# Sums by src four steps ahead, id loads on ScalarE's queue and four-step loops in a graph kernel's joint stage; bonds ahead of rows in its sort

## The reference

```python
feat_in  = h @ W_in.T + b_in;   feat_out = h @ W_out.T + b_out
a_in  = seg_mean(feat_in[src], dst, N)      # mean over the edges that end at a node
a_out = seg_mean(feat_out[dst], src, N)     # mean over the edges that begin at a node
x = layernorm(x + gru_cell(concat(a_in, a_out), h))
# second layer
m = relu(concat(h[row], h[col], bond) @ W1 + b1) @ W2 + b2
x = layernorm(x + h + segment_sum(m * sigmoid(bond @ Wa + ba), row))
```

## Time and profile before

| | |
|---|---|
| median of three runs | 13765.5 us (13765.47, 13765.5, 13784.85) |
| profiled execution | 13790.1 us, its span 13788.4 us |
| mean granted TensorE clock | 0.751 of full speed |
| busy share: PE, PEld, DVE, ACT, POOL | 63%, 56%, 61%, 20%, 70% |
| `sort_records`, first to last POOL scatter | 2369.1 to 6652.3 us |
| `sum_rest`, first gather to last DVE row | 6675.7 to 8843.2 us |

### The profile page before, as it was taken

How to read it: one execution, slowest core, us unless ns; L and a number is a source line. 1 busy time by engine, 2 the same in 40 slices (tenths; PEclk the granted TensorE clock), 3 DMA queues, 4 the chain that set the end, 5 groups by cost and what they waited for, 6 DMA issues and landing times. The chain is left out here.

```text
span 13788.4 us, 248865 instructions
## 1 busy us (share of the span) xinstructions
PE 8650.6 (63%) x53687; PEld 7661.1 (56%) x53688; DVE 8351.6 (61%) x29389; ACT 2713.3 (20%) x7251; POOL 9705.6 (70%) x10125
## 2 busy tenths in 40 slices
PE   3777776333333333333577777797888888888876
PEld 2555554333333333333577777556777777777775
DVE  6555555666666666666677777554444455444444
ACT  0000000111111111111000000154444444444444
POOL 3777776777777777777777777306777777777774
PEclk9555555555656555666788888898999999999998
DMA  5822223666666666666677777513333334333336
GB/s 178 308 54 54 54 54 84 197 198 196 199 196 199 197 199 196 199 196 199 174 187 186 186 186 186 95 52 76 80 79 79 80 88 94 80 79 80 79 79 82
DMA packets 2665496, 1884.08 MB, mean 137 GB/s; under 512 B 1375795, under 2 KB 2460371, under 8 KB 2664784
## 3 DMA queue, kind: packets, MB, share of 16 engines
q1 hardware_dynamic: 1505269, 806.75, 22.1%
q0 software_dynamic: 377360, 782.89, 19.9%
q10 hardware_dynamic: 782662, 292.60, 8.8%
HBM read 1509.53 MB, written 483.44 MB: 145 GB/s over the span
## 5 line engine op out<-in xcount | busy, mean ns | idle before, releaser
L1846 POOL DMA_INDIRECT p<-q_rows,small x3432 | 3250.1, 947 | 1643.5 <-issue 1000.0
L1051 PE MATMUL bank<-p,ring 128*128 x6656 | 1549.0, 426 | 2714.7 <-DVE ring L972 2711.5
L1051 PEld LDWEIGHTS bank<-p,ring 128*128 128x128 f32 x6656 | 1437.8, 328 | 2826.1 <-issue 2826.1
L1110 POOL DMA_INDIRECT edges_a<-ring,small x1664 | 1635.7, 983 | 563.1 <-issue 441.4
L1110 POOL DMA_INDIRECT edges_b<-ring,small x1664 | 1632.5, 981 | 507.6 <-issue 441.1
L799 POOL DMA_INDIRECT ring<-in_x,ring x1664 | 1573.9, 946 | 533.7 <-issue 530.0
L1884 PE MATMUL bank<-ring 128*128 128x256 f32 x3432 | 1205.4, 437 | 766.4 <-DVE p L1796 766.1
L830 PE MATMUL bank<-ring 128*128 128x129 f32 x3328 | 1240.3, 491 | 617.8 <-DMA ring<-in_x,ring 525.1
L1252 POOL DMA_INDIRECT ring<-in_x,small x1352 | 1278.7, 946 | 463.2 <-issue 411.3
L1272 PE MATMUL bank<-p,ring 128*128 128x129 f32 x8360 | 1194.3, 312 | 525.1 <-DVE ring L1200 525.1
L1272 PEld LDWEIGHTS bank<-p,ring 128*128 128x128 f32 x8360 | 1157.7, 226 | 562.5 <-issue 562.5
(11 more groups left out here) (289 smaller groups left out, 14195.4 us busy)
## 6 DMA issues: line engine op xcount, KB each, us to landing
p<-rows_by_slot SPq DMA_DIRECT2D x418, 928.0 KB
p<-edges_b SPq DMA_DIRECT2D x530, 262.0 KB
p<-edges_a SPq DMA_DIRECT2D x520, 262.0 KB
bonds_by_dst<-in_bond ACTq DMA_DIRECT2D x5, 20625.0 KB, 159.1
ring<-edges_a ACTq DMA_DIRECT2D x1792, 33.0 KB
p<-q_rows,small POOLq DMA_INDIRECT x3432
ring<-edges_b ACTq DMA_DIRECT2D x1664, 33.0 KB
ring<-bonds_by_dst ACTq DMA_DIRECT2D x1672, 32.0 KB
```

The source lines that it names most:

```text
L1051: last = nc.tensor.matmul(found[q][:, j, :], hot_t[g % GRPS][:, QUAD * h + j, :], x, start=True, stop=True, skip_group_check=True)
L1110: pool.indirect_dma_start(out=c.edges[s], out_offset=bass.IndirectOffsetOnAxis(ap=pos[:, k:k + 1], axis=0), in_=rec[:, k, :], in_offset=No ...
L1846: pool.indirect_dma_start(out=gath[g][:, k, :], out_offset=None, in_=c.q_dram, in_offset=bass.IndirectOffsetOnAxis(ap=gidx[g][:, k:k + 1], ...
```

## The change

In the sort, SP's order within a step is turned: the bonds' wait and load come first, then the rows'.

In the joint stage:

- PE and DVE run the sums by src four steps ahead of the sums by dst (`LEAD`): before the loop PE makes `sum_out` of steps 0 to 4, and DVE `add_out` of steps 0 to 3 with the preparations that follow; a turn has `add_in(u)`, `add_out(u + 4)`, `prepare_in(u + 2)`, `prepare_out(u + 6)`.
- PE's and DVE's loops have four steps; the last two turns (eight steps) are written out, without the work that lies beyond step 207.
- DVE loads the block numbers of a step in two parts, eight before `add_in`, five before `add_out`.
- The ids to gather and the places in the block are loaded by ScalarE's queue in two DMAs, the places into four buffers of their own. ScalarE waits for the last gather of step u - 3, then for DVE's `prepare_in(u)`.
- `sum_out` is zeroed by ScalarE (an activation with scale 0). POOL no longer waits for any zeroing.
- SP has only the windows; the two loads of windows past the last step are gone.

```diff
@@ sort_records, SP
                         u = i * LOOK + g
+                        sp.wait_ge(s_sc[2 * (g % GRPS)], i * (2 * QUAD * 16) + g // GRPS * (QUAD * 16))
+                        load_bonds(u, 2 * (g % GRPS))
                         sp.wait_ge(s_hot, u * 4 + 12)
                         load_rows(u + 2, g % 2)
-                        sp.wait_ge(s_sc[2 * (g % GRPS)], i * (2 * QUAD * 16) + g // GRPS * (QUAD * 16))
-                        load_bonds(u, 2 * (g % GRPS))
@@ sum_rest
-    W, AHEAD = D + 1, 5
+    s_blank = c.sem("s_blanked")
+    W, AHEAD, LEAD = D + 1, 5, 4
+    TURNS_S = QSTEPS // TURN_V          # TURN_V = 4
@@ SP
                     for g in range(LOOK):
-                        u = i * LOOK + g
-                        load_windows(u, g % 2, edges)
-                        sp.wait_ge(s_agg_in, u * NI + (IN_0 - (LOOK - AHEAD - 1) * NI))
-                        load_ids(u + AHEAD, (g + AHEAD) % LOOK)
-            for k in range(2):
-                load_windows(QSTEPS + k, k, c.edges[1])
+                        load_windows(i * LOOK + g, g % 2, edges)
@@ DVE
-            nc.vector.memset(c.sum_out, 0.0).then_inc(s_zero, 1)
+            def turn(i, g, most=QSTEPS):
+                u = i * TURN_V + g
+                add_in(u, blocks_in(u))
+                if g + LEAD < most:
+                    add_out(u + LEAD, g, blocks_out(u + LEAD))
+                if g + 2 < most:
+                    prepare_in(i, (g + 2) % TURN_V, (g + 2) // TURN_V)
+                for h in range(NO):
+                    if g + LEAD + 2 < most:
+                        prepare_out(i, (g + LEAD + 2) % TURN_V, h, (g + LEAD + 2) // TURN_V)
...
+            dve.wait_ge(s_blank, 1)
+            for v in range(LEAD):
+                add_out(v, v, blocks_out(v))
+                for h in range(NO):
+                    prepare_out(0, (v + 2) % TURN_V, h, (v + 2) // TURN_V)
+            with dve.Fori(0, TURNS_S - 2) as i:
+                for g in range(TURN_V):
+                    turn(i, g)
+            for i in range(TURNS_S - 2, TURNS_S):
+                for g in range(TURN_V):
+                    turn(i, g, QSTEPS - i * TURN_V)
@@ ScalarE, new
+            for g in range(AHEAD):
+                load_ids(g, g)
+            for n in range(TURN_V):
+                load_locals(n, n)
+            nc.scalar.activation(c.sum_out.rearrange("p b d -> p (b d)"),
+                                 c.ones_f[:, 0:1].to_broadcast([P, (NB + 1) * W]), ACT.Copy, scale=0.0).then_inc(s_blank, 1)
+            with act.Fori(0, QSTEPS // LOOK) as i:
+                for g in range(LOOK):
+                    u, last = i * LOOK + g, (g - 3) % GRPS * HALF + HALF - 1
+                    act.wait_ge(s_g[last], i * (16 * LOOK // GRPS) + 16 * ((g - 3) // GRPS + 1))
+                    load_ids(u + AHEAD, (g + AHEAD) % LOOK)
+                    act.wait_ge(s_hot_in, u + 1)
+                    load_locals(u + TURN_V, g % TURN_V)
@@ POOL
-            pool.wait_ge(s_zero, 4)
@@ PE
-            sum_out(0, 0)
-            with pe.Fori(0, QSTEPS // LOOK) as i:
-                for g in range(LOOK):
+            for v in range(LEAD + 1):
+                sum_out(v, v)
+            with pe.Fori(0, TURNS_S - 2) as i:
+                for g in range(TURN_V):
                     sum_in(i, g)
-                    sum_out(i * LOOK + (g + 1), (g + 1) % LOOK)
+                    sum_out(i * TURN_V + (g + LEAD + 1), g + LEAD + 1)
```

More of the change, by code:

```diff
@@ L1141, in sum_rest @@
     lo_out = c.small[:, 24:24 + QPS * QW]
-    ids = [c.small[:, 128 + n * 2 * HALF:128 + (n + 1) * 2 * HALF].rearrange("p (f k) -> p f k", k=HALF) for n in range(LOOK)]
+    ids = [c.small[:, 128 + n * HALF:128 + (n + 1) * HALF] for n in range(LOOK)]
+    local = [c.small[:, 256 + n * HALF:256 + (n + 1) * HALF] for n in range(TURN_V)]
     out_bank = [c.bank[0:2], c.bank[2:4]]
@@ L1160, in load_windows @@
                                      ).then_inc(s_win[2 * g + h], 16)
-            for g in range(AHEAD):
-                load_ids(g, g)
             for n, edges in enumerate(c.edges):
@@ L1180, in _ @@
             nc.vector.memset(far[:, :, D:W], 1.0).then_inc(s_zero, 1)
-            nc.vector.memset(c.sum_out, 0.0).then_inc(s_zero, 1)
             nc.vector.tensor_copy(c.iota_p, c.iota).then_inc(s_zero, 1)
-            dve.wait_ge(s_zero, 4)
+            dve.wait_ge(s_zero, 3)
             def prepare_in(i, g, ahead=0):
                 a, b = g % 2 * HALF, (g % 2 + 1) * HALF
-                dve.wait_ge(s_ids[g], 16 * i + (16 * ahead + 16))
-                nc.vector.tensor_tensor(hot_in[:, a:b, :], ids[g][:, 1, :].unsqueeze(2).to_broadcast([P, HALF, P]),
+                dve.wait_ge(s_loc[g], 16 * i + (16 * ahead + 16))
+                nc.vector.tensor_tensor(hot_in[:, a:b, :], local[g].unsqueeze(2).to_broadcast([P, HALF, P]),
                                         c.iota_p.unsqueeze(1).to_broadcast([P, HALF, P]), ALU.is_equal).then_inc(s_hot_in, 1)
@@ L1225, in _ @@
                     prepare_out(0, g, h)
+            for g in range(2):
                 prepare_in(0, g)
[L1227 to L1236, removed]
@@ L1237, in _ @@
-            step.end(QSTEPS // LOOK)
+            dve.wait_ge(s_blank, 1)
[4 more added lines that the diff above has]
+            with dve.Fori(0, TURNS_S - 2) as i:
+                step.loop(i, TURN_V * NO)
+                for g in range(TURN_V):
+                    turn(i, g)
+            step.end(TURNS_S - 2)
+            for i in range(TURNS_S - 2, TURNS_S):
+                for g in range(TURN_V):
+                    turn(i, g, QSTEPS - i * TURN_V)
@@ L1238, in _, with load_ids, load_locals @@
             dve.wait_ge(s_acc_in, HS + ADDED_IN_0)
             dve.wait_ge(s_acc_out, QSTEPS * QPS + ADDED_OUT_0)
+        @block.scalar
+        def _(act):
+            def load_ids(u, g):
+                act.dma_start(ids[g], c.slots_d[:, bass.ds(u + B_GROUP, 1), GATHER * HALF:(GATHER + 1) * HALF]
+                             .rearrange("p o w -> p (o w)")).then_inc(s_ids[g], 16)
+            def load_locals(u, n):
+                act.dma_start(local[n], c.slots_d[:, bass.ds(u + B_GROUP, 1), LOCAL * HALF:(LOCAL + 1) * HALF]
+                             .rearrange("p o w -> p (o w)")).then_inc(s_loc[n], 16)
+            for g in range(AHEAD):
[11 more added lines that the diff above has]
+                    load_locals(u + TURN_V, g % TURN_V)
+            for g in range(LOOK):
+                act.wait_ge(s_ids[g], 16 * (QSTEPS // LOOK + (1 if g < AHEAD else 0)))
+            for n in range(TURN_V):
+                act.wait_ge(s_loc[n], 16 * (QSTEPS // TURN_V + 1))
+            act.wait_ge(s_blank, 1)
```

36 lines of the change are left out of this document (21 added, 15 removed).

## The result

The changed kernel takes 13820.8 us (median of 7 runs, 13815.6 to 13826.6) against 13771.4 (7 runs, 13765.5 to 13784.9) for the kernel before: ratio 1.0036, 95% interval 1.0027 to 1.0045, some 49 us slower. I had said 13725, a range of 13690 to 13772, and "slower" at 0.10.

A forecast was written before the change was run, and what follows sets the result against it. DVE was taken to bound the joint stage, at 10.15 us a step; its end was to move from 8843.2 to 8803, 40 us less, taken off the median 13765.5 to give 13725, range 13690 to 13772.

The forecast's parts named there:

- the price of the load between the sums: Joint stage, DVE: the load of five block numbers before the sums by src is exposed, adding 0.40 us a step.
- rival (b): Joint stage: load of five costs as much as eight, or prologue drags; 10.44 us a step, no change, 13763; chance 0.16.
- the end: Last steps of the joint stage: DVE could end at 8787, one-row gathers and windows make the DMA last, at 8803.
- rival (d): Joint stage's end: windows for the last four steps land late, DVE waits 13 us twice; 14 less, 13751; chance 0.12.
- The reading of the clog: Joint stage's end: the last 56 gathers read one row of x, at 1.45 us of DMA time each against 0.24.
- the jump: DVE's loop, joint stage: four-step body cuts the jump's idle from 3.2 us per eight steps to 0.25 a jump; gain 0.40 - 0.02 a step.
- turn 0: Joint stage's start: after four rounds of sums by src and preparations, DVE's turn 0 starts near 6703 (6697 to 6712).
- zeroing: Joint stage's start: ScalarE zeroes 12771 values instead of DVE, in at most 12.6 us, done by about 6677.
- POOL's first gather as cover: Joint stage's start: POOL starts about 6665 instead of 6675.73, which is no gain while DVE is last.
- nothing lost by ScalarE's queue: Joint stage: loading ids and local rows on ScalarE's queue adds nothing, to 1 us at the start.
- Sort: Sort stage: issuing bonds ahead of rows changes nothing, bounds plus and minus 8 us.
- rival (a): Joint stage: the load of five is hidden, DVE runs 9.77 a step and catches POOL; 69 less, 13696; chance 0.17.

## Why the prediction was wrong

*Failed: the price of the load between the sums.* The step "So 0.40 us a step come in. Bounds: 0 (hidden), and 0.67 (dear as eight)". The mechanism was right (exposed, since the sums before it wait for one another), the size was not. Measured from start to start (8726.29 - (8722.17 + 3.32 - 0.29) = 1.09, less 0.34) it is 0.75 a step, even above my upper bound. Of the 0.35 that were missing, 0.23 to 0.30 are the load, which I had scaled with its number of values (0.30 to 0.37; it took 0.60), and 0.08 the rest around it (0.49, where I took the 0.41 of the earlier trace rows). With 0.75, the pace is 9.77 + 0.75 = 10.52, as seen (10.53), though two small misses cancel in it (below). Over 200 steps 0.36 a step is 72 us: the forecast's 40 and more. It was rival (b)'s mechanism at a price beyond its bound, and DVE, not the DMA, ended last.

*Half right: the end.* I took the windows to be through when DVE's last full steps came. They weren't: 24 us of waits (9.57 and 14.48), rival (d)'s. The two added up, where I had each alone. From the predicted step 200: 8737, less 17 for the earlier start, plus 72 for the pace, 24 for the windows and 2 for the prologue gives 8818; the trace has 8819.8. The reading of the clog itself held: spreading the rows took 30 us and more away, in both kernels.

*Right in its cause, a little short in its size: the jump.* The body of eight steps brings its idle back. But the short body's jump costs 0.33 us (1.47 from L1191's start to the sum's at 8711.62, 1.14 at 8722.17) and the hole behind it 0.13 more: 0.12 a step, where the sum had 0.02. The gain is 0.28 a step, not 0.38. A step without a jump takes 10.42, which is 9.68 + 0.74: the small losses that I had put into 9.75 are gone, and hid the miss. The straight code from step 200 on begins without an idle (8819.79), but behind a wait of 14.48, so that its fetching is not priced. Also right: turn 0 at 44 us (42 forecast); zeroing at 10.85 us (at most 12.6); POOL's first gather as cover that brings nothing while DVE is last (up to 8800 us PE's sums end POOL's idle ahead of 174 gathers, 2.9 us at the longest); nothing lost by ScalarE's queue, as POOL waits for ids only once, at the start.

*Sort: right within its bounds.* 8 us, where I said nothing within 8; its start, which I had not looked at, brought them. The last scatter came 17 us earlier in the profile, beyond the 8 that I had named as a sign of being wrong. The rest of the 17 is not the edit's: 3.9 were there before the sort began, and the mean scatter, of which there are 3328, differs by up to 4 ns from one execution to another (980 to 984).

*The sum.* By the profile I had said 13750, and the profiled execution took 13818.6: 69 us more, as the stage ended at 8871.8 and not at 8803. The other 27 of the 96 between 13725 and the median are the step from the profile to the median: before's profiled execution was a long one among its runs, and I took its 24.6 off the forecast; the changed kernel's lay 2 below its median. Ordering decided the result: the same edits with the load beside L1179 gave 13706, not far from rival (a)'s 13696, "the load is hidden".

## What to carry to other kernels

A load of block numbers on the sequencer costs nothing only if a long enough operation is in flight behind which it runs: here the load plus 0.4 to 0.5 us must fit (0.60 behind 1.21 does, 1.09 behind 1.22 leaves 0.36). After a chain of short operations that wait for one another all of it shows, once in every step; splitting such a load, or moving work across it, needs its place counted before its length. A row that every padding entry reads is a hot row: spread it, above all where other transfers share the queues.

## What the runs showed of the hardware

- A register load from SBUF on DVE goes by steps and by place: one value 0.32 us, five or eight at a multiple of four words 0.60, 13 at such a place 1.09, five at an odd one 1.18. SP's loads of five, at places 0, 5, 10, ..., took 0.52 in two steps of eight and 1.07 in the others. Around a load DVE's sequencer spent another 0.49 us between the two sums.
- A loop body of 236 instructions on DVE jumps back in 0.25 us of idle and fetches hardly any code again (2 packets of the instruction queue in 810 us); bodies of 451 to 471 fetch five or six packets of 8 KB a turn and idle 1.7 to 4.6 us in the joint stage. The sort's body of 365 idles nothing. Where the limit lies, and whether the place of a body counts, stays open.
- Gathers of one and the same row take 1.54 us of the 16 DMA engines each, against 0.25 for spread rows of equal size: about six times.
- A wait's name is the last semaphore's: the same hole of 0.79 us was put down to PE in half of the steps and to issue in the others, and went whole when the load moved.
- What stays open: why an odd place doubles the load's price, and whether the rule is four words or another alignment (only places of 0, 5, 8, 9 and their like were tried).
